# Flamingo block on one core: order of the copies and stores in the context stage, and another bank for the last query block

## The reference

```python
x = x + tanh(g_xattn[0]) * matmul(fake_quant(ln(x)), fake_quant(ctx))          # quantised product
x = x + tanh(g_ffn[0])   * (quant_per_token(ln(x)) @ dequant(W_int).T + bias)  # int8 layer
x = x + tanh(g_xattn[1]) * attention(ln(x), ctx, ctx; Wq, Wk, Wv, Wo)          # 32 query heads, 8 key heads
x = x + tanh(g_ffn[1])   * (ln(x) @ dequant_fp4(packed).T)
```

## Time and profile before

| what | us |
|---|---|
| median of 3 runs | 857.45 (855.44 to 859.82) |
| the profiled execution, its own time | 856.11 |
| its span, first to last instruction | 854.3 |
| TensorE busy in the span | 823.5 (96%) |
| VectorE, ScalarE, GpSimd busy | 594.9, 448.8, 535.1 |
| mean granted clock of TensorE, as a share of the full one | 0.994 |

### The profile page before, as it was taken

One profiled execution on the slowest core, in us unless ns is written; L12 is line 12 of the kernel. 1 busy time (PEld: TensorE's weight loads), 2 busy tenths in 40 slices (PEclk: granted clock), 3 DMA queues, 4 the chain that ended last, 5 costly groups with the idle time before them and its releaser, 6 DMA issues.

```text
span 854.3 us, 14034 instructions
## 1 busy us (share of the span) xinstructions
PE 823.5 (96%) x4498; PEld 332.7 (39%) x4498; DVE 594.9 (70%) x850; ACT 448.8 (53%) x741; POOL 535.1 (63%) x235
## 2 busy tenths in 40 slices
PE   8997989899999999999999999999999889999998
PEld 7665744344444432222222232222222213444443
DVE  6876779988388577888878888888888500555622
ACT  4434466565322157677767777777777772111200
POOL 6645157966343428888889888888988885211200
PEclk9998999999999999999999999999999999999999
DMA  7999955337995215455465455456544434122331
GB/s 254 252 282 274 232 129 137 78 86 126 242 236 157 84 59 115 102 106 115 96 133 124 96 111 117 102 114 132 114 102 99 90 64 94 25 51 49 61 136 74
DMA packets 120822, 107.81 MB, mean 126 GB/s; under 512 B 85324, under 2 KB 105804, under 8 KB 116684
## 3 DMA queue, kind: packets, MB, share of 16 engines
q1 hardware_dynamic: 115120, 71.59, 32.3%
q0 software_dynamic: 4608, 33.56, 19.4%
q10 hardware_dynamic: 1052, 2.10, 0.9%
HBM read 41.55 MB, written 12.58 MB: 63 GB/s over the span
## 4 chain that ended last, share of the span: by engine, by line
PE 53%; POOL 13%; DMA 12%; DVE 9%; issue 6%; DVEq 3%; ACT 3%; ACTq 0%; POOLq 0%; SPq 0%
POOL wraw L601 10%; DMA tail<-wraw 8%; PE mpair L1608 6%; PE sbank L1668 6%; PE sbank L1677 6%; PE sbank L1478 4%; PE sbank L1480 4%; PE sbank L1479 4%; PE sbank L1744 3%; PE sbank L1761 3%; PE sbank L1748 3%; PE sbank L1759 3%; PE sbank L1746 3%; DVEq L953 3%; DMA regD<-wraw 3%
## 5 line engine op out<-in xcount | busy, mean ns | idle before, releaser
L1340 DVE TENSOR_REDUCE mx<-mpair 128x1 f32<-128x1024 f32 x256 | 302.2, 1216 | 62.0 <-PE mpair L1608 61.0
L895 ACT ACTIVATE regC<-sbank 128x512 f32<-128x512 f32 x512 | 277.9, 594 | 106.2 <-PE sbank L1668 102.0
L1668 PE MATMUL sbank<-regD 98*128 98x512 f16 x512 | 178.3, 384 | 7.8 <-ACT regC L895 5.6
L601 POOL TENSOR_TENSOR wraw<-regC 128x2048 f32<-128x2048 f32 x32 | 148.8, 4649 | 31.5 <-DMA tail<-wraw 26.7
L1608 PE MATMUL mpair<-regD 96*128 96x512 f16 x512 | 155.9, 380 | 1.0 <-DVE mx L1340 0.4
L1677 PE MATMUL sbank<-regC,regD 128*32 128x512 f32 x1024 | 136.4, 605 | 1.0 <-ACT regC L895 1.0
L1668 PEld LDWEIGHTS sbank<-regD 98*128 98x128 f16 x512 | 48.5, 97 | 186.2 <-ACT regC L895 146.0
L601 POOL TENSOR_TENSOR regD<-regC 128x2048 f32<-128x2048 f32 x16 | 76.5, 4784 | 15.1 <-ACT regC L895 15.1
L601 POOL TENSOR_TENSOR tail<-regC 128x2048 f32<-128x2048 f32 x16 | 77.0, 4814 | 0.0
L1608 PEld LDWEIGHTS mpair<-regD 96*128 96x128 f16 x512 | 47.6, 98 | 54.4 <-DVE mx L1340 13.9
L494 POOL TENSOR_SCALAR xT_lo<-xT_lo,sc 128x1024 f32<-128x1024 f32 x16 | 30.3, 1895 | 41.6 <-DVE X L1005 34.7
(11 more groups left out here) (185 smaller groups left out, 1287.6 us busy)
## 6 DMA issues: line engine op xcount, KB each, us to landing
regD<-wraw POOLq DMA_DIRECT2D x16, 1024.0 KB, 7.0
tail<-wraw POOLq DMA_DIRECT2D x16, 1024.0 KB, 7.0
xT_lo<-in_ctx SPq DMA_DIRECT2D x16, 512.0 KB, 4.7
wraw<-in_L_ffn_W_int SPq DMA_DIRECT2D x8, 512.0 KB, 4.3
X<-in_x SPq DMA_DIRECT2D x4, 1024.0 KB, 6.8
wraw<-in_L_xattn_Wq SPq DMA_DIRECT2D x8, 512.0 KB, 3.7
wraw<-in_L_xattn_Wo SPq DMA_DIRECT2D x8, 512.0 KB, 4.2
regD<-q_hi_scratch SPq DMA_DIRECT2D x32, 128.0 KB, 2.4
```

What stands on the lines that cost most here:

```text
L601: nc.gpsimd.tensor_tensor(p_sum[pr if pr < 3 else 1][:, :, :], probs[:, (2 * pr) % 4, :, :], probs[:, (2 * pr) % 4 + 1, :, :], ALU.add).th ...
L895: nc.scalar.activation(probs[:, kt % 4, h, :], bank[4 + h % 2], ACT.Exp, scale=SCALE).then_inc(s["exp_ok"], 1)
L1340: v.tensor_reduce(mx[m][:, bass.ds(n, 1)] if par is not None else mx[m][:, n:n + 1], slot[:, :, :], AX.XY, ALU.max).then_inc(s["mx_red"], 1)
L1668: pe.matmul(bank[4 + h % 2], kst[par][0:98, kt * P:(kt + 1) * P], qst[par][0:98, h * 512:(h + 1) * 512], start=True, stop=True).then_inc(s ...
```

## The change

It moves instructions in the lists of SP, ScalarE and VectorE, adds one instruction on ScalarE, and gives one block of the query projection another bank. Nothing else is computed.

- SP: `store_k(c - 1)` stands ahead of the first turn of the chunk.
- ScalarE and VectorE: the copies of turned tile 12 move from the head of chunk 2 into chunk 1, among the first norm's passes. `k_out(c, 1)` and `k_low(c, 1)` move ahead of the second norm tile, and `ctx_high(u + 3)` ahead of `ln1_root`.
- Last chunk: `ln1_root(3)` moves ahead of `k_out(3, 0)`, and VectorE's `ln1_affine(3)` ahead of `k_low(3, 0)`; `wd_high(7)` ahead of `ln1_affine(6)`; VectorE's `ln1_round(7)` ahead of `k_low(3, 1)`.
- ScalarE makes one Exp of a single column behind the second query block.
- The last query block goes to bank 6. The first two scores both wait for the block but one; the wait for the last block's low part moves to the first `pv`.

```diff
--- before.py
+++ after.py
@@ -221,6 +221,9 @@
+        def q_bank(b, blk, par):
+            return bank[6] if (b, blk) == (B - 1, KD - 1) else bank[4 + par]
+
         ITEMS = S * REP // P
         LEAD = 8
         NPAIR = KT // 2
@@ -317,9 +320,9 @@
 
             for c in range(NCH - 1):
                 u = TB * (c + 1)
-                ctx_turn(u + 1)
                 if c > 0:
                     store_k(c - 1)
+                ctx_turn(u + 1)
                 if u + TB < U:
                     load_ctx(u + TB)
                 ctx_turn(u + 2)
@@ -754,8 +757,6 @@
 
             def chunk(c):
                 u = TB * (c + 1)
-                if c > 1:
-                    turned_high(u, 6)
                 ctx_high(u + 1)
                 v_out(c, 0, False)
                 v_out(c, 1, False)
@@ -765,13 +766,15 @@
                 v_out(c, 3, False)
                 k_out(c, 0, False)
                 wd_high(2 * c + 1)
+                ctx_high(u + 3)
                 ln1_root(c - 1)
-                ctx_high(u + 3)
                 ln1_affine(2 * c - 2)
+                if u + TB < U:
+                    turned_high(u + TB, 6)
                 ln1_out(2 * c - 2)
+                k_out(c, 1, False)
                 ln1_affine(2 * c - 1)
                 ln1_out(2 * c - 1)
-                k_out(c, 1, False)
 
             first_chunk()
             for c in range(1, NCH - 1):
@@ -786,13 +789,13 @@
             v_out(c, 3, False)
             ln1_out(T - 4)
             ln1_affine(T - 3)
+            ln1_root(c)
             k_out(c, 0, False)
             ln1_out(T - 3)
-            ln1_root(c)
             for n in range(2 * B):
                 c2_out(n)
+            wd_high(T - 1)
             ln1_affine(T - 2)
-            wd_high(T - 1)
             ln1_out(T - 2)
             ln1_affine(T - 1)
             k_out(c, 1, False)
@@ -874,12 +877,14 @@
                 act.wait_ge(s["q_mm"], KD * b + blk + 1)
                 if not first:
                     act.wait_ge(q_st[par], 32 * (KD // 2 * b + blk // 2))
-                nc.scalar.activation(kq_hi[:, par, :], bank[4 + par], ACT.Copy, scale=1.0 / WS).then_inc(s["q_hi"], 1)
+                nc.scalar.activation(kq_hi[:, par, :], q_bank(b, blk, par), ACT.Copy,
+                                     scale=1.0 / WS).then_inc(s["q_hi"], 1)
 
             y3_out(6)
             q_high(0, 0, 0, True)
             y3_out(7)
             q_high(0, 1, 1, True)
+            nc.scalar.activation(sd[:, 0:1], EPSC, ACT.Exp)
             for n in range(2, 2 * KD):
                 q_high(n // KD, n % KD, n % 2)
                 if n in WO_AFTER:
@@ -1144,8 +1149,6 @@
 
             def chunk(c):
                 u = TB * (c + 1)
-                if c > 1:
-                    turned_low(u, 6)
                 ctx_low(u + 1)
                 ctx_round(u)
                 wd_low(2 * c)
@@ -1163,9 +1166,11 @@
                 ctx_round(u + 2)
                 ln1_round(2 * c - 2)
                 wd_scale(2 * c + 2)
+                if u + TB < U:
+                    turned_low(u + TB, 6)
+                k_low(c, 1)
                 ln1_round(2 * c - 1)
                 ctx_round(u + 3)
-                k_low(c, 1)
                 d()
 
             first_chunk()
@@ -1179,12 +1184,12 @@
             ln1_round(T - 4)
             ln1_stats(c)
             ln1_round(T - 3)
+            ln1_affine(c)
             k_low(c, 0)
-            ln1_affine(c)
+            wd_low(T - 1)
             ln1_round(T - 2)
-            wd_low(T - 1)
+            ln1_round(T - 1)
             k_low(c, 1)
-            ln1_round(T - 1)
 
             def bias_scale():
                 dve.wait_ge(s["bias_in"], 16)
@@ -1308,7 +1313,7 @@
 
             def q_low(b, blk, par):
                 dve.wait_ge(s["q_hi"], KD * b + blk + 1)
-                v.scalar_tensor_tensor(out=kq_lo[:, par, :], in0=bank[4 + par], scalar=1.0 / WS,
+                v.scalar_tensor_tensor(out=kq_lo[:, par, :], in0=q_bank(b, blk, par), scalar=1.0 / WS,
                                        in1=kq_hi[:, par, :], op0=ALU.mult, op1=ALU.subtract).then_inc(s["q_lo"], 1)
 
             def unpack(w, first=False):
@@ -1615,7 +1620,7 @@
                     pe.wait_ge(s["ab_ev"], 4 * T - 4)
                 else:
                     pe.wait_ge(s["q_lo"], KD * b + blk - 1)
-                three(bank[4 + par], lambda k: wq_hi[:, k, bass.ts(blk, P)], lambda k: wq_lo[:, k, bass.ts(blk, P)],
+                three(q_bank(b, blk, par), lambda k: wq_hi[:, k, bass.ts(blk, P)], lambda k: wq_lo[:, k, bass.ts(blk, P)],
                       lambda k: xT_hi[:, k, b * S:(b + 1) * S],
                       lambda k: xTl[:, k, b * S:(b + 1) * S], between).then_inc(s["q_mm"], 1)
 
@@ -1662,7 +1667,7 @@
             def score(g, par, kt, h, first):
 
                 if first and kt == 0 and h < 2:
-                    pe.wait_ge(s["q_lo"], 2 * KD - 1 + h)
+                    pe.wait_ge(s["q_lo"], 2 * KD - 1)
                 else:
                     pe.wait_ge(s["exp_ok"], 32 * g + 4 * kt + h - 1)
                 pe.matmul(bank[4 + h % 2], kst[par][0:98, kt * P:(kt + 1) * P],
@@ -1671,7 +1676,9 @@
             def pv(g, par, kt, first=False):
 
                 pe.wait_ge(s["exp_ok"], 32 * g + 4 * kt + 4)
-                if kt == 0 and not first:
+                if kt == 0 and first:
+                    pe.wait_ge(s["q_lo"], 2 * KD)
+                elif kt == 0:
                     pe.wait_ge(s["acc_ev"], g)
                 for h in range(REP):
                     m = pe.matmul(bank[6][HD * h:HD * h + HD, :], vst[par][:, kt * HD:(kt + 1) * HD],
```

## The result

The changed kernel takes 852.03 us (median of 6 runs, 850.95 to 853.60) and the kernel before 857.53 us (6 runs). The ratio is 0.9931, 95% interval 0.9917 to 0.9945: 5.9 us faster (4.7 to 7.1) by the ratio, 5.5 by the medians. The profiled execution took 850.95 us with a span of 849.1, against 856.11 and 854.3. It is faster and inside the range. It is 4.3 us above the forecast of 847.7, between the two times given for rival A (850.6 and 853.7).

A forecast was written before the change was run, and what follows sets the result against it. The prediction took the context stage to be bound by TensorE's hole and the late copying engines, the attention moving as a whole; 8.5 (term 2, including term 1) + 1.3 (term 3) = 9.8 us, 857.45 to 847.7, range 843.2 to 852.8.

The forecast's parts named there:

- rival A: Context stage: the copying engines do not follow TensorE, only 3.0 us ahead; time 850.6, or 853.7 with nothing followed; chance 0.15.
- The sum of 9.8 us: Whole kernel: 8.5 us by the start of `stage_ab(1)` plus 1.3 us where the attention begins.
- its own sign of being wrong: End of the context stage: prediction wrong if `stage_ab(1)` starts after 121, or if stage AB takes longer than before.
- term 3: Start of the attention: the early Exp takes the table load before the first exponential off the path, 1.3 us.
- term 2: End of the context stage: `stage_ab(1)` starts at 117.8 instead of 126.26, 8.5 us gained, term 1 included.
- Term 1: TensorE's hole before `wd_turn(4)`: costs 8.5 us, closes except 0.9 us waiting for tile 11; 7.6 us gained.
- the copying engines run 6.0 ahead from there on: From `ctx_high(15)`: it waits about 1.6 us for tile 13, so ScalarE and VectorE keep 6.0 of TensorE's 7.6 us.
- Term 2's first half: Last chunk, ScalarE: the 3.71 us wait at `ln1_affine(6)` goes, so `k_out(3, 1)` starts at 115.2 instead of 124.90.
- Term 2's second half: Last chunk, VectorE: `ln1_round(7)` ahead of `k_low(3, 1)` adds 1.2 us; `stage_ab(1)` starts at 117.8, TensorE waits 1.5.
- the following: Context stage: the copying engines coming earlier behind TensorE, forecast at 6.0 us with bounds 3.0 and 7.6.

The follow-up runs named there:

- `k_low` first: The changed kernel with VectorE's `k_low(3, 1)` ahead of `ln1_round(7)` again: 849.40 us, ratio 0.9904 to the kernel before.
- `k_out` early: The changed kernel with `k_low(3, 1)` ahead of `ln1_round(7)` and ScalarE's `k_out(3, 1)` ahead of `ln1_out(6)`: 849.89 us, ratio 0.9910.
- tile 12 alone: The kernel before with only tile 12's copies moved into chunk 1 on ScalarE and VectorE: 857.61 us, ratio 1.0002.
- last chunk alone: The kernel before with only the new order of the last chunk on ScalarE and VectorE: 855.87 us, ratio 0.9969.
- the pair: The kernel before with only the early Exp and the last query block in bank 6: 854.59 us, ratio 0.9961.
- context part alone: The changed kernel without the early Exp and the other bank, so only the context stage's reordering: 852.57 us, ratio 0.9939.
- tile 12 and key store: The kernel before with tile 12's copies moved and SP's key store ahead of the turn, nothing else: 855.47 us, ratio 0.9979.

## Why the prediction was right, and where it was wrong

It was right on the sign and its range holds the time. The sum of 9.8 us was too large by about 4, and its parts erred in both directions. By its own sign of being wrong, a `stage_ab(1)` later than 121, its account of the context stage failed: it started at 122.53, 3.7 us earlier than before in place of 8.5. What happened is in the main rival A, which had a chance of 0.15. That the range holds the time is partly luck: the median is 0.8 us inside its slow end, and term 3, timed at 2.0 more than forecast, made up for part of what term 2 missed.

**Term 1 was right at its place and worth little.** The hole closes and tile 11 makes TensorE wait 0.98 us (0.9 predicted). `k_out(1, 0)` starts at 56.45 (54.7 predicted), in an execution that began 1.8 us late (last section); with `k_low` first, where the start was not late, it is 54.96. `stage_ab(0)` starts 5.4 us earlier in the one and 5.7 in the other, where 7.6 were given. And tile 12's move alone gained nothing, and taking it back out cost nothing. TensorE's lead is not what sets the end of the stage.

**The failed step: "the copying engines run 6.0 ahead from there on".** They run 3.1 ahead at `ln1_affine(4)` (4.1 with `k_low` first and 3.1 with `k_out` early, whose lists are the same up to there). The prediction looked for the gate at tile 13's landing in front of `ctx_high(15)`; that one did not wait. It gave 3.0 as the lower bound, and rival A was worked out from it. The gate that the profiles show is the load of x tiles 4 and 5, further down SP's queue: VectorE's statistics wait 1.28 us for its landing. And that load is late because SP's list is full. Its rows just ahead of it:

```profile
85.15 1.59 SPq L275 DMA_DIRECT2D v_scratch<-vtmp  x1
86.84 2.94 SPq L260 DMA_TRANSPOSE regC<-X  x1
89.83 1.31 SPq L262 DMA_TRANSPOSE regC<-X  x1
91.19 0.58 SPq L252 DMA_DIRECT2D wraw<-in_L_ffn_W_int  x1
```

and, in the kernel before, the same store and the transpose behind it:

```profile
85.07 0.44 SPq L272 DMA_DIRECT2D v_scratch<-vtmp  x1
90.46 1.59 SPq L257 DMA_TRANSPOSE regC<-X  x1
```

Before, SP stood still for 4.95 us, until `ctx_high(15)` was done. In the changed kernel each issue follows the last within 0.12 us from 39.21 to the load at 91.81. So it is in all eight kernels of the table that have the moved key store: the load comes 52.6 to 55.9 us behind the first issue of that row, in whatever order, VectorE waits 1.28 to 2.21 us for it, and `ln1_affine(4)` starts 11.6 to 12.2 us behind its issue, while `wd_turn(4)` ranges from 67.24 to 71.31. In the three others (before, tile 12 alone, last chunk alone) `ln1_affine(4)` starts 11.9 to 12.3 us behind the load as well, but there VectorE does not wait for it: SP waits 2.9 to 5.0 us for `ctx_high(15)`, and ScalarE's list is the gate. Whenever the edits opened one wait on the way there, the next in the queue held (the key store, tile 13, the weight tile of `wd_scale(6)`). No run moved the load itself or took an issue out of SP's list, and none moved the key store alone, so how much a shorter list would give stays open.

**Term 2's first half was right but for 0.9.** The wait of 3.71 us vanished, because the columns came before GpSimd's additions, and the last chunk alone gained 2.7 us. From `ln1_affine(4)` to `ln1_affine(6)` 2.8 us came of it: `wd_high(7)`, 1.09 us, now stands in front.

**Term 2's second half was mis-sized.** `ln1_round(7)` in front of `k_low(3, 1)` was taken at 1.2 us. The time from `k_out(3, 1)` to `k_low` grew from 0.61 to 2.48, by 1.87, and rounding 6 cost another 0.3. This is where the prediction had weighed a rule of the Trainium skill ("SBUF — State Buffer", section "SBUF: two separate sides"), that an instruction of GpSimd holds the ports it shares with VectorE to its end, and left it out of the sum. The rows agree with the rule, and show its form: the additions run from 111.60 at 12.48 / 5 = 2.5 us each, so two of them end at 116.6 and 121.6; the two roundings issued at 115.00 (1.81 us) and 119.44 (2.44 us) end at 116.8 and 121.9. Each ends just behind the addition that was under way. The wait left at `stage_ab(1)` is then 3.90 in place of 1.5. Its start, 4.7 us later than the 117.8 forecast, is made up of 2.9 (the following), 0.9 (`wd_high(7)`), 0.3 (rounding 6) and 0.7 (rounding 7).

**Stage AB moved as a whole, and by two limits.** From `stage_ab(1)` to the query projection it takes 85.7 us, 85.6 before. But the start of that block is only one of two limits. In the profiles the query projection starts 80.2 to 80.6 us behind the end of `stage_ab(1)`'s products, or 83.9 to 84.2 behind VectorE's first copy of the stage, whichever is later; all fourteen profiles fit, but the two numbers were read from them and no run was made to test them. The changed kernel hangs on the first, 122.53 + 5.31 + 80.4 = 208.2 (208.26 measured), `k_low` first on the second, 120.82 + 84.1 = 204.9 (204.84). That is why an earlier `k_out(3, 1)` gave nothing.

**Term 3 was mis-sized.** 1.3 us were forecast, with the bank at nothing and 0.5 taken back without it. The profiles give 1.4 between the last product of the query projection and the first exponential, and the pair timed 3.3. The rest is TensorE's clock in front of the first sums, which stayed at 1.00 in the one profile that the prediction had: 9.13 - 7.55 = 1.6 us. By the rule of the Trainium skill weighed there ("ScalarE: Activation LUTs", section "What ACT_TABLE_LOAD costs"), a drain beside each switch of tables, the estimate was 2.7, near the timed gain. Yet no row shows the drain, and the clock accounts for the difference.

What stays open: the gains of the last chunk alone (2.7) and of the pair (3.3) add up to 6.0, the whole of the changed kernel. The 3.1 us at `ln1_affine(4)`, by which the copying engines do come earlier, should stand beside them. In single profiles they do. In the medians the context part alone (5.2) is 2.5 above the last chunk alone (2.7), but the intervals overlap (3.1 to 7.3 and 1.6 to 3.7), and this kernel's start varies.

## What to carry to other kernels

When a stall is closed, follow the queue that feeds the engine behind it to the end of the stage, and not only to the next wait: here SP issues everything in one order, and three edits in a row only changed which of its transfers was waited for. Look in that queue for gaps first: where each issue follows the last at once, as over 52.6 us here, another order brings one transfer earlier and the others later. Before a pass is put in front of a short copy for which TensorE waits, look whether GpSimd is at work on the same stretch: the same pass took from 1.35 to 2.44 us, by how far the addition under way had still to go, and the short copy 0.69 in any case. And a term read from one profile is no better than that profile: where a short pause of TensorE stands in it, look in a second execution whether the clock held.

## What the runs showed that I had not expected

- The length of a wait alone does not say whether TensorE keeps its clock. At `stage_ab(1)` the 16 products took 5.31 us behind waits of 2.24, 3.90 and 4.24 us (before, changed, tile 12 and key store), but 3.63 us behind 3.03 us in the context part alone (one profile), and 3.63 behind 1.87 and 1.35.
- The start of the program varies. The first two float32 turns in TensorE's timeline, in the changed kernel and before:

```profile
11.66 1.91 PE L1456 MATMUL mpair<-id,xT_lo 128*128 128x128 f32 x8
14.75 1.04 PE L1456 MATMUL sbank<-id,xT_lo 128*128 128x128 f32 x8
```

```profile
10.75 1.04 PE L1451 MATMUL mpair<-id,xT_lo 128*128 128x128 f32 x8
12.93 1.04 PE L1451 MATMUL sbank<-id,xT_lo 128*128 128x128 f32 x8
```

  The list of TensorE is the same up to there. The first turn ran at the lower clock in one execution, and the second came 1.8 us later. In the kernel with the context part alone the two start at 12.02 and 14.74, with `k_low` first at 10.28 and 12.46, so it belongs to no edit.
